# Two-layer mixture residual by two identity matmuls, one-layer residual on Pool, and a new order of the work

## The reference

```
x = x + 0.5 * ffn0(ln(x))     # MOE0_A: 16 experts, two layers each (128 -> 256 -> 128), exact gelu
x = x + attn0(ln(x))          # ATT0
x = x + 0.5 * ffn0(ln(x))     # MOE0_B, same weights as MOE0_A
x = x + 0.5 * ffn1(ln(x))     # MOE1_A: 16 experts, one layer each (128 -> 128), relu
x = x + attn1(ln(x))          # ATT1: causal linear attention, running sums within a sequence
x = x + 0.5 * ffn1(ln(x))     # MOE1_B, same weights as MOE1_A

ffn0(t) = t + sum_e comb[t,e] * (gelu(t @ W1[e] + b1[e]) @ W2[e] + b2[e])    # comb: top 2 of a softmax
ffn1(t) = sum_e w[t,e] * relu(t @ We[e] + be[e])                             # w: top 2 of a softmax
```

## Time and profile before

| | |
|---|---|
| median of 3 runs | 738.96 us |
| profiled execution, its own time | 736.88 us |
| its span | 735.2 us |
| PE busy | 656.1 us (89%) |
| DVE busy | 509.0 us (69%) |
| ACT busy | 403.9 us (55%) |
| POOL busy | 214.4 us (29%) |
| chain that ended last | PE 38%, DVE 25%, issue 19%, POOL 11%, ACT 6% |

### The profile page before, as it was taken

The page is one execution under the profiler, slowest core; times in us unless marked ns, Lnnn a source line. Parts: engine busy times, 40 slices in busy tenths (PEclk is TensorE's granted clock), DMA queues, the critical chain, the costliest instruction groups (busy, mean ns, idle before and its releaser), DMA issues.

```text
span 735.2 us, 7595 instructions
## 1 busy us (share of the span) xinstructions
PE 656.1 (89%) x2395; PEld 417.7 (57%) x2395; DVE 509.0 (69%) x1139; ACT 403.9 (55%) x795; POOL 214.4 (29%) x148
## 2 busy tenths in 40 slices
PE   3699998999999999999999998999999869868693
PEld 2456565555555565665666665566666445555472
DVE  5587457647446636658599687869776468688887
ACT  4254464546545544766754695584476325745394
POOL 2120010110002202181320364041037136775367
PEclk9899998999999999999999999999999969989897
DMA  8772522053243134512223232103221000000001
GB/s 244 153 152 63 111 58 58 20 97 58 60 105 66 59 68 79 73 26 46 58 58 70 48 58 58 57 3 91 72 41 27 1 0 0 1 0 16 14 1 29
DMA packets 27027, 42.23 MB, mean 57 GB/s; under 512 B 1689, under 2 KB 8938, under 8 KB 26986
## 3 DMA queue, kind: packets, MB, share of 16 engines
q1 hardware_dynamic: 26986, 41.74, 26.5%
HBM read 40.42 MB, written 1.31 MB: 57 GB/s over the span
## 4 chain that ended last, share of the span: by engine, by line
PE 38%; DVE 25%; issue 19%; POOL 11%; ACT 6%; DMA 0%; SPq 0%; DVEq 0%; POOLq 0%; ACTq 0%
PE py L1103 14%; PE ph L882 4%; PE ph L883 4%; PE ph L884 4%; POOL stage L440 3%; POOL rstd L387 3%; POOL stage L444 3%; DVE xn L659 2%; DVE red L769 2%; DVE hw L841 2%; ACT stage L528 2%; DVE stage L766 1%; DVE stage L736 1%; DVE X L771 1%; PE ps L1057 1%
## 5 line engine op out<-in xcount | busy, mean ns | idle before, releaser
L577 ACT ACTIVATE g<-ph,b1col 128x512 f32<-128x512 f32 x256 | 171.9, 689 | 146.6 <-PE ph L884 111.8
L1103 PE MATMUL py<-hw,w2s 128*128 128x512 f32 x512 | 249.0, 611 | 2.4 <-DVE hw L841 2.4
L841 DVE TENSOR_TENSOR hw<-g,bc 128x1024 f32<-128x1024 f32 x128 | 166.1, 1301 | 94.7 <-ACT g L577 93.2
L387 POOL TENSOR_TENSOR rstd<-vare,mhalf 128x4 f32<-128x4 f32 x24 | 36.6, 1524 | 392.2 <-DVE vare L653 392.2
L1103 PEld LDWEIGHTS py<-hw,w2s 128*128 128x128 f32 x512 | 97.6, 194 | 78.5 <-issue 64.9
L882 PE MATMUL ph<-xbh,w1h 128*128 128x512 f32 x256 | 135.1, 528 | 0.0
L528 ACT ACTIVATE stage<-ps,comb 128x128 f32<-128x128 f32 x288 | 84.1, 514 | 44.4 <-PE ps L1013 28.5
L883 PE MATMUL ph<-xbl,w1h 128*128 128x512 f32 x256 | 103.4, 404 | 0.0
L884 PE MATMUL ph<-xbh,w1l 128*128 128x512 f32 x256 | 103.3, 404 | 0.0
L882 PEld LDWEIGHTS ph<-xbh,w1h 128*128 128x128 f32 x256 | 49.9, 195 | 28.5 <-issue 20.6
L883 PEld LDWEIGHTS ph<-xbl,w1h 128*128 128x128 f32 x256 | 50.1, 196 | 24.0 <-issue 17.0
(11 more groups left out here) (207 smaller groups left out, 959.7 us busy)
## 6 DMA issues: line engine op xcount, KB each, us to landing
bc<-comb_rows SPq DMA_DIRECT2D x31, 1024.0 KB, 8.5
stage<-in_L_ffn_W_dram SPq DMA_DIRECT2D x4, 512.0 KB, 6.9
X<-in_L_attn_x_dram SPq DMA_DIRECT2D x4, 256.0 KB, 3.3
bc<-comb_rows SPq DMA_DIRECT2D x4, 256.0 KB, 5.6
out_dram<-X SPq DMA_DIRECT2D x4, 256.0 KB, 2.3
comb_rows<-combT SPq DMA_DIRECT2D x8, 32.0 KB, 2.1
side<-in_L_attn_wq_dram SPq DMA_DIRECT2D x1, 64.0 KB
side<-in_L_attn_wk_dram SPq DMA_DIRECT2D x1, 64.0 KB
```

The source lines that it names most:

```text
L387: nc.gpsimd.tensor_tensor(rstd[:, 0:n], vare[:, 0:n], mhalf[:, 0:n], ALU.pow).then_inc(light["rstd"], 1)
L577: nc.scalar.activation(g[:, s % 2, h, 0:w], ph[:, (HC * s + h) % RING_PH, 0:w], ACT.Gelu, bias=b1col[:, HC * e + h:HC * e + h + 1]).then_i ...
L841: V.tensor_tensor(hw[:, s % RING_HW, :, 0:w], g[:, s % 2, :, 0:w], bc[:, s // GQ % 2, s % GQ, 0:w].unsqueeze(1).to_broadcast([P, HC, w]), ...
L1103: ins = T.matmul(py[:, 0:cols], w2s[:, w], hw[:, s2 % RING_HW, h, 0:cols], start=e2 == 0 and h == 0, stop=False)
```

## The change

Four things change.

1. **The two-layer residual** goes from POOL to PE. With the first expert of each of the 8 passes, two float32r matmuls with an identity (`ident_r`) put `xbh` and `xbl` of that chunk into `py`. POOL's two instructions and the wait in `c0` go.
2. **The one-layer mixture** is split otherwise. `ACT_GROUPS` is 4 in the heavy stream (ACT does all 16 experts) and 3 in the late one. The heavy stream's halving is one POOL add of 1024 columns; the late stream keeps two adds of 512. The third add (L444 on POOL, L766 on DVE) goes: DVE reduces 8 to 1 in one instruction. The 0.5 is in the router's weights, and the add to `X` is POOL's, 128 columns per tile, with a buffer of two sums (`red`).
3. **Small router values** (`lgs`, `oh1`, `selm`, `topf`, `s_rec`) lie in the unused half of the PSUM bank `pl` and no more in SBUF; the next light step on PE therefore waits for `comb`, not for `shift`.
4. **The order**: `TURNS` is new on every engine, and in the light stream c1 of MOE0_A comes before c2.

```diff
-    ACT_GROUPS = 3
+    ACT_GROUPS = (4, 3)
...
+    QUARTERED = {(MOE1_A, 0): False, (MOE1_B, 0): False, (MOE1_A, 1): False, (MOE1_B, 1): False}
...
-        lgs, shf, exs = (sb(n, [P, TPC, E]) for n in ("lgs", "shf", "exs"))
+        shf, exs = (sb(n, [P, TPC, E]) for n in ("shf", "exs"))
...
+        small = pl[:, CH // 2:CH]
...
-                if moe0(l):
-
-                    pool.wait_ge(light["xn"], nth_light("xn", l, c))
-                    if last:
-                        pool.wait_ge(*last.pop())
-                    nc.gpsimd.tensor_scalar(xnh[:, 0:wide(c)], xn[:, 0:wide(c)], 0.5, 1.0, ALU.mult, ALU.mult).then_inc(pool_step, 1)
...
-                    nc.gpsimd.tensor_tensor(X[:, col(c)], X[:, col(c)], xnh[:, 0:wide(c)], ALU.add).then_inc(light["res"], 1)
...
+                def residual(j):
+                    pool.wait_ge(signal["sum"], n + j + 1)
+                    nc.gpsimd.tensor_tensor(X[:, tile_(c, j)], X[:, tile_(c, j)], total[:, (n + j) % 2, :], ALU.add).then_inc(signal["red"], 1)
...
+                    if acts == GROUPS:
+                        pool.wait_ge(signal["relu_a"], (n + j + 1) * acts)
+                        both, other = (r[:, j % 2, a * E * D // 2:(a + 1) * E * D // 2] for a in range(2))
+                        nc.gpsimd.tensor_tensor(both, both, other, ALU.add).then_inc(signal["half"], 2)
...
+                    if j:
+                        residual(j - 1)
+                        yield
+                residual(ntiles(c) - 1)
...
-                                act.wait_ge(signal["red"], n + j - 1)
+                                act.wait_ge(signal["sum"], n + j - 1)
...
-                        (klink if late else hlink)(V.tensor_tensor(r0, r0, r2, ALU.add))
...
-                    ins = V.scalar_tensor_tensor(xs_, sum_[:, :], 0.5, xs_, ALU.mult, ALU.add)
-                    ins.then_inc(signal["red"], 1)
...
+                        V.tensor_reduce(sums, r[:, j % 2, 0:E * D // 2].rearrange("p (a d e) -> p d a e", a=2, d=D), mybir.AxisListType.XY, ALU.add).then_inc(signal["sum"], 1)
...
-                    signal = {"ln": "xl", "rt": "shift", "ct": "ct"}[last]
+                    signal = {"ln": "xl", "rt": "comb", "ct": "ct"}[last]
...
+                    if e2 == 0:
+                        T.matmul(py[:, 0:cols], ident_r[:, :], xbh[:, col(MAIN[n2][1])], start=True, stop=False)
+                        T.matmul(py[:, 0:cols], ident_r[:, :], xbl[:, col(MAIN[n2][1])], start=False, stop=False)
```

More of the change, by code:

```diff
@@ L84, in build_program @@
         mhalf = sb("mhalf", [P, TPC])
-        ones_r, tri_r = sb("ones_r", [P, P], f32r), sb("tri_r", [P, P], f32r)
+        ones_r, tri_r, ident_r = (sb(n, [P, P], f32r) for n in ("ones_r", "tri_r", "ident_r"))
         w1h, w1l = sb("w1h", [P, E * H], f32r), sb("w1l", [P, E * H], f32r)
@@ L156, in build_program @@
         ps = ctx.enter_context(nc.psum_tensor("ps", [P, 3, CH], f32))
+        small = pl[:, CH // 2:CH]
+        lgs, oh1, selm = (small[:, i * TPC * E:(i + 1) * TPC * E].rearrange("p (t e) -> p t e", t=TPC) for i in range(3))
+        topf = small[:, 3 * TPC * E:3 * TPC * E + 2 * TPC].rearrange("p (t a) -> p t a", t=TPC)
+        s_all, s_rec = (small[:, 3 * TPC * E + i * TPC:3 * TPC * E + (i + 1) * TPC] for i in (2, 3))
         def by_tile(buffer, i):
@@ L203, in build_program @@
                                           "vz", "o_ps", "o", "x")}
-        f1 = {(l, late): {n: sem(f"f{l}_{late}_{n}") for n in ("y_ps", "relu_a", "relu_v", "half", "quarter", "red")}
+        f1 = {(l, late): {n: sem(f"f{l}_{late}_{n}") for n in ("y_ps", "relu_a", "relu_v", "half", "quarter", "sum", "red")}
               for l in (MOE1_A, MOE1_B) for late in (0, 1)}
@@ L263, in nth_light @@
             stage_ = STAGE_OF.get(signal, "ln")
-            same = [t for t in LIGHT if t[0] == stage_ and (signal != "res" or moe0(t[1]))]
+            same = [t for t in LIGHT if t[0] == stage_]
             return same.index((stage_, l, c)) + 1
@@ L442, in f1_ @@
-                    if l == MOE1_A:
+                    if acts == GROUPS:
+                        pool.wait_ge(signal["relu_a"], (n + j + 1) * acts)
+                        both, other = (r[:, j % 2, a * E * D // 2:(a + 1) * E * D // 2] for a in range(2))
+                        nc.gpsimd.tensor_tensor(both, both, other, ALU.add).then_inc(signal["half"], 2)
+                    else:
+                        pool.wait_ge(signal["relu_a"], (n + j + 1) * acts)
+                        nc.gpsimd.tensor_tensor(r0, r0, r2, ALU.add).then_inc(signal["half"], 1)
+                        pool.wait_ge(signal["relu_v"], (n + j + 1) * (GROUPS - acts))
+                        nc.gpsimd.tensor_tensor(r1.rearrange("p (d e) -> p d e", d=D), r1.rearrange("p (d e) -> p d e", d=D),
+                                                r3.rearrange("p (e d) -> p d e", d=D), ALU.add).then_inc(signal["half"], 1)
@@ L443, in f1_ @@
+                    if QUARTERED[l, late]:
                         pool.wait_ge(signal["half"], 2 * (n + j + 1))
-                        nc.gpsimd.tensor_tensor(r0, r0, r2, ALU.add).then_inc(signal["quarter"], 1)
+                        nc.gpsimd.tensor_tensor(r0, r0, r1, ALU.add).then_inc(signal["quarter"], 1)
                     yield
+                    if j:
+                        residual(j - 1)
+                        yield
+                residual(ntiles(c) - 1)
+                yield
@@ L515, in f1_ @@
                 banks, r = (ph, rel_late) if late else (ps, rel)
+                acts = ACT_GROUPS[late]
                 act.wait_ge(light["comb"], nth_light("comb", l, c))
@@ L747, in f1_ @@
                 late, signal, n = moe1(l, c)
-                banks, r, sum_ = (ph, rel_late, red_late) if late else (ps, rel, red)
+                banks, r, total = (ph, rel_late, red_late) if late else (ps, rel, red)
+                acts = ACT_GROUPS[late]
                 for j in range(ntiles(c)):
                     for q in range(GROUPS):
-                        if q >= ACT_GROUPS:
+                        if q >= acts:
                             if j == 0:
@@ L760, in f1_ @@
                         yield
-                    if l == MOE1_A:
+                    if n + j >= 2:
+                        dve.wait_ge(signal["red"], n + j - 1)
+                    sums = total[:, (n + j) % 2, :]
+                    if QUARTERED[l, late]:
                         dve.wait_ge(signal["quarter"], n + j + 1)
+                        V.tensor_reduce(sums, r[:, j % 2, 0:E * D // 4].rearrange("p (d e) -> p d e", d=D), AX, ALU.add).then_inc(signal["sum"], 1)
                     else:
                         dve.wait_ge(signal["half"], 2 * (n + j + 1))
-                        r0, r2 = (r[:, j % 2, a * E * D // 4:(a + 1) * E * D // 4] for a in (0, 2))
-                        (klink if late else hlink)(V.tensor_tensor(r0, r0, r2, ALU.add))
-                    if j:
-                        dve.wait_ge(signal["red"], n + j)
-                    (klink if late else hlink)(V.tensor_reduce(sum_[:, :], r[:, j % 2, 0:E * D // 4].rearrange("p (d e) -> p d e", d=D), AX, ALU.add))
-                    xs_ = X[:, tile_(c, j)]
-                    ins = V.scalar_tensor_tensor(xs_, sum_[:, :], 0.5, xs_, ALU.mult, ALU.add)
-                    ins.then_inc(signal["red"], 1)
+                        V.tensor_reduce(sums, r[:, j % 2, 0:E * D // 2].rearrange("p (a d e) -> p d a e", a=2, d=D), mybir.AxisListType.XY, ALU.add).then_inc(signal["sum"], 1)
                     yield
@@ L1100, in main @@
                     cols = wide(MAIN[n2][1])
+                    if e2 == 0:
+                        T.matmul(py[:, 0:cols], ident_r[:, :], xbh[:, col(MAIN[n2][1])], start=True, stop=False)
+                        T.matmul(py[:, 0:cols], ident_r[:, :], xbl[:, col(MAIN[n2][1])], start=False, stop=False)
                     for h in range(HC):
                         w = slice((e2 * HC + h) * D, (e2 * HC + h + 1) * D)
-                        ins = T.matmul(py[:, 0:cols], w2s[:, w], hw[:, s2 % RING_HW, h, 0:cols], start=e2 == 0 and h == 0, stop=False)
+                        ins = T.matmul(py[:, 0:cols], w2s[:, w], hw[:, s2 % RING_HW, h, 0:cols], start=False, stop=False)
                     ins.then_inc(slot_done, 1)
```

44 lines of the change are left out of this document (17 added, 27 removed), and 37 rows, old and new, of the table TURNS.

## The result

| | before | after |
|---|---|---|
| median of 4 runs each, on one chip | 741.49 us | 708.16 us (701.82 to 710.03) |
| ratio, 95% interval | | 0.954 [0.9457, 0.9622] |
| profiled execution, its span | 736.88, 735.2 us | 708.15, 706.4 us |
| last main matmul (main's end) | 584.8 us | 571.1 us |
| tail, from there to the end | 150.4 us | 135.3 us |

The change is faster by 4.6%. Of the 28.8 us between the two spans the tail gave 15.0 and main 13.8, where I had expected a loss of 5.7 in main.

The account below looks back on a forecast made before the run. PE was taken to bound the main stretch and a chain of waits the tail; main's end 590.6 plus tail parts 53, 38 and 41 gave 722.6 us of span, with 1.7 around it 724.3, range 710 to 740.

Parts of the forecast that it names:

- Main: Stretch up to the last main matmul: 3.7 us for identity matmuls plus 2 for ACT's relus, ending at 590.6.
- The other order of c1 and c2 and the start: Main stretch: the new order and the start change nothing, 0 us, between -2 and +2.
- ACT's fourth group: Main stretch: ACT takes the fourth relu group of 12 heavy tiles; 2 us, between 0 and 13.3.
- POOL's residual: Main stretch: removing POOL's 16 residual instructions gains 0, since nobody but `c0` waits for them.
- The identity matmuls: Main stretch: 16 added 512-column matmuls on PE cost 3.7 us, between 3.7 and 6.9.
- Tail A: Main's end to ATT1's input for c3: 53 us against 65.3 before, as 18 + 15 + 20.
- Tail B: ATT1 of c3, with less DVE work: 38 us against 41.9 before, between 34 and 42.
- Tail C: MOE1_B of c3 with the store, closed by ACT: 41 us against 43.1 before.
- The small router values: Router values moved to PSUM: 0 us.
- The tail keeps its length: Rival: the tail is chains of waits and stays at 147 us, time 739; chance 0.27.
- `hw` blocked: Rival: in main, POOL's longer add blocks DVE's `hw` and PE with it, main +24 us, time 749.5; chance 0.11.
- ACT fills the tail: Rival: ACT's work alone sets the tail, 113.5 us, time 706; chance 0.08.

Follow-up runs that it names:

- e13: Changed kernel with three heavy-stream relu groups on ACT, the fourth on DVE, and POOL halving in two 512-column adds; 717.5 us, ratio 0.9653.
- e9: Kernel before, with identity matmuls on PE in place of POOL's residual and nothing else changed; 737.8 us, ratio 0.9951.
- e3: Changed kernel with POOL's residual back in place of the identity matmuls; 703.5 us, ratio 0.9493.
- e10: Same code as e3, measured a second time with more rounds; 704.3 us, ratio 0.9485.
- e14: Changed kernel with DVE doing two of each tile's four relu groups, not one, in MOE1_B of c3; 710.0 us, ratio 0.9577.
- e11: Changed kernel with the small router values in SBUF again and the next light step on PE waiting for `shift`; 713.5 us, ratio 0.9614.
- e18: Changed kernel with third add, DVE's add to `X` and three relu groups on ACT restored, new order kept; 736.6 us, ratio 0.9927.
- e6: Changed kernel with each identity matmul issued four times, making the residual four times too large; 718.1 us, ratio 0.9692.

## Why the prediction was wrong

**Main, -13.8 for a forecast of +5.7: the failed step.** The step read "there only work on PE counts" and then "The other order of c1 and c2 and the start: 0, between -2 and +2". PE's 3.8 idle us of 80 in the earlier trace rows were taken for the floor. Over all of main they are 40.3 us, and the earlier trace rows had the largest name for them, `xn`, 22.2 us over the span. 16.2 of it lay in main, and no term of the sum stood for it. The order alone takes 10.0 us of the idle time away, the code alone 5.8, both 19.1; 13.0 of these are `xn`. In my sum for main no term could fall by more than 2 us, and I gave none of them a fall. The forecast's main end of 590.6 was 19.5 us too late, its tail of 132 was 3.3 too short, and the two make the 16.2 us by which 724.3 missed 708.15.

**ACT's fourth group, +2, and POOL's residual, 0.** Both were wrong in sign. With three groups in the new order PE is idle 4.8 us longer (26.0 against 21.2, e13), so the move to ACT, with POOL's single add that comes with it, gave some 5. And e9 shows that in the old order POOL's residual did cost: without it the waits for `xn` in main fell by 3.3 and the idle time by 4.9; in the new order they differ little with it and without (e3, e10). The identity matmuls, +3.7, were near at 3.3.

**Tail A, 53 forecast, 55.1.** Weights +19.0 (forecast 18). Last relu 19.3 behind them (15). ATT1's input 16.8 behind that (20); the prices in it held: 2.39 for the 1024-column add (2.4), 1.22 for the reduce (1.22), 0.47 for the 128-column add (0.5). By the Trainium skill (GPSIMD Engine Reference, 4.1 Engine selection) the last would have been 0.58, an estimate, and the trace has it at 0.47.

**Tail B, 38 forecast, 39.8. Tail C, 41 forecast, 40.4.** C came out nearly as forecast for a reason that was half right: ACT's relus have hardly a gap, but giving one group of each tile to DVE in e14 gained nothing. The whole tail, 132 forecast, is 135.3. **The small router values, 0 forecast,** are worth 3.1 us of it (e11). By the Trainium skill (SBUF — State Buffer, Who interferes with whom) a DVE instruction with two SBUF inputs contends with a GpSimd instruction that reads SBUF, and one with at most one SBUF input, outside the two-port modes, does not. The trace agrees: 0.583 us on average with two SBUF operands, 0.224 with one in PSUM. I used the rule for `hw` alone.

**Rivals.** *The tail keeps its length* is false for the whole change and true for each half of it (150.5 with the code alone, 158.4 with the order alone); its reason, chains of waits, is seen in e18. *`hw` blocked* is false as a cost: PE waits for it 0.3 us. Single ones are long (up to 2.77 us, before as after), but the mean is 1.30 in both. *ACT fills the tail* named the right time, 706, by the wrong way: its tail was 113.5 behind a main that ends at 590.6.

## What to carry to other kernels

Where the fullest engine stands at 93 to 95% of a stage, the missing 5 to 7% are a term of the sum: list its waits in that stage by name and ask of each whether the change moves it. An order and the code it was made for are one change: tried apart, as placed here, they gave 0.6 and 0.8%, together 4.6%; and a part that paid before (the identity matmuls) has to be tried again in the end, where it cost some 0.6%. In a loop through a two-deep buffer, ask what stands between the last write and the release, and take out first what the next writer doesn't need (here the add to `X`).

## What the runs showed of the hardware that was not expected

The kernel before ran, over 17 executions beside e6, between 735.06 us at a mean granted clock of 0.955 and 745.54 at 0.937: some 10 us for 0.018. e14's profile shows the same in one stretch: the main code of the changed kernel, at a granted clock of 0.99 in place of 0.98, has PE busy for 543.5 us and not 549.9, and ends at 565.1 and not at 571.1. So a station of one profile is good to some 6 us in main here, while PE's idle time was within 1.9 us in repeats of the same code (21.2 and 22.4; 21.7 and 23.6). The profiled execution of before (736.88) lies at the short end of this range, at 0.955, so the spans differ by 28.8 us and the medians by 33.3.

The stalls of `shf` are the other finding. A DVE instruction of 0.22 us with both operands in SBUF took up to 2.25 us beside POOL's 1024-column add (e11), and with one operand in PSUM it was never above 0.225 us in sixteen times.
